# Swin block with a mixture of experts on one core: one order of work for all engines replaced by a table for each engine, one product moved to GpSimd

## The chip, the cores and the metric

One NeuronCore of one Trainium2 chip runs the whole program. The metric is the device time of one execution in microseconds (us), from the first to the last instruction with what lies around them. Engines are named as the profile names them: PE (TensorE, the matmuls; PEld its weight loads), DVE (VectorE), ACT (ScalarE), POOL (GpSimd) and SP (SyncE, which here only issues DMAs).

## The reference

The input is 16 images of 56x56 positions with 32 channels, in float32. Two residual blocks follow each other:

```
x = x + window_attention(layernorm(x))      # 7x7 windows, shifted by 3, 4 heads of 8 channels
x = x + experts(layernorm(x))               # 8 experts of 32x32, the best 2 of each position

attention: q, k, v = h @ w_qkv + b_qkv
           a = softmax(q k^T * 8**-0.5) + bias + mask   # bias and mask come after the softmax
           out = (a v) @ w_proj + b_proj
experts:   p = softmax(h @ router_w + router_b); the two largest p, divided by their sum
           out = p1 * (h @ We1 + be1) + p2 * (h @ We2 + be2)
```

## The kernel before

**Units.** The work is cut into 16 units. A unit is half the columns of two images, 4 columns of windows by 8 rows of windows by 2 images: 64 windows, in 112 partitions of x and 28 windows' columns by 32 channels along the free axis. Every unit passes through the same steps, each step a function of the name in the tables:

- `load` (SP, 12 DMAs into the single tile `xin`), `keep` (SP, one DMA from `xin` to `x_kept`, of which there are two), `kept` (POOL, adds the projection's bias to `x_kept`).
- `norm1_center`, `norm1_square`, `norm1_scale`, `norm1_root`: the first layernorm, which goes DVE (sum, L893), POOL (centre, L558), ACT (square), DVE (sum), ACT (logarithm and exponential), DVE (root), POOL (scale, L567). `norm2_*` does the same for the second one.
- `xt`, `q`, `k`, `v`: PE turns the rows and projects them, ACT copies the results to SBUF. `place` and `kmask` spread q and k by heads (POOL L593 and L630, ACT L733). `ob` is bias and mask times v.
- Attention runs in four groups g of 16 windows. For each: `maximum` (PE products into `ps_win`, L1213; DVE maximum of each row, L943, and its split, L957 and L959), `shift` (PE turns the maxima, L1221; ACT copies them to `mr`, L778), `scores` (PE, L1236 and L1242, into the same `ps_win`; ACT exponential to `pt`, L788), `pv` (PE products with v, L1258; DVE divides by the sums, L966 and L970; POOL adds `ob`, L601). There is one `ps_win`, so `maximum` of a group can't start before the exponentials of the group before it are read out.
- `ot`, `y`, `back`: PE turns and projects, DVE adds `x_kept` (L984) and so makes `x2`.
- `x2t`, `route`, `logits`: PE and ACT. `top2` picks the two largest in six pieces: pieces 0 to 4 on DVE (L999 to L1034), piece 5 on POOL. `share` turns the shares of the experts.
- `replicate` (SP): the normed tokens are copied by DMA to the four groups of partitions (tile `x4`). `gates` (SP): shares go to DRAM in 4 DMAs and come back spread over partitions in 8 DMAs, 4 for experts 0 to 3 (semaphore `gates_low`) and 4 for experts 4 to 7 (`gates_high`).
- `mul` (DVE, L1046): four products of `gates` with `x4`, pieces 0 to 3; pieces 0 and 2 are 448 columns wide and 1 and 3 are 336, times 4. Pieces 0 and 1 use the low experts, 2 and 3 the high ones. `sum` (PE) adds the experts in `ps_acc`, `mix_drain` (ACT), `final` (PE, DVE L1054), `store` (SP, 12 DMAs).

**Order.** All five engines walk one list, `program()`: each engine takes from it the steps in which it has a part, in that order, and runs them strictly one after the other. The list is a prologue, then for each unit one macro step with places (g, 0) to (g, 3), where `SIDE_TASKS` says which steps of other units stand, then a tail. In the macro step of unit n, attention is that of n, `xt` to `ob` and `keep` that of n+1, `load` and the first norm that of n+2, `y` to `top2` piece 2 that of n-1, the rest that of n-2. `back` stands at places (0, 2) and (0, 3), `keep` ahead of it at (0, 0), `load` at (0, 1), `norm1_center` of the next unit at (1, 0), and `maximum` of group 2 after it.

`keep` of unit n+1 waits until `back` of unit n-1 has read the same `x_kept`, and `load` waits until `keep` has emptied `xin`:

```
sp.wait_ge(token_drained, upto("token_drained", v.before(2), 1))      # keep
sp.wait_ge(x_kept_ready, upto("x_kept_ready", v.before(1)))           # load
dve.wait_ge(x_loaded, upto("x_loaded", v))                            # norm1_center on DVE
```

PE's small products share two PSUM banks in turn (`FILL_ORDER`): a fill waits until the fill two before it is read out.

## Time and profile before

| | |
|---|---|
| median of 3 runs | 995.84 us (995.42 to 998.39) |
| the profiled execution's own time | 994.43 us |
| its span, first to last instruction | 992.6 us |
| busy share of the span | PE 67%, PEld 43%, DVE 59%, ACT 38%, POOL 40% |
| mean granted TensorE clock | 0.753 of full speed |
| DMA moved | 100.79 MB, mean 102 GB/s |

No engine is busy for much over two thirds of the span. The busy time of PE depends on the clock that it was granted, since the same matmuls take longer at the lower one. The chain that ended last passes through PE for 34% of the span, DVE 23%, DMA 14%, "issue" (time in which the engine waited for nothing that the profile shows) 10%, ACT 8% and SP's queue 7%.

### The profile page before, as it was taken

What the parts mean: (1) busy time and instruction counts of PE and PEld (TensorE: products, weight loads), DVE (VectorE), ACT (ScalarE), POOL (GpSimd) and SP (SyncE); (2) the same over time, 40 slices, a digit from 0 to 9 for tenths busy, and PEclk for the clock granted to TensorE, in tenths of its full rate; (3) what the DMA queues carried; (4) which work ended last, traced back from release to release, by engine and by line L of the source; (5) the groups of instructions that cost most, each with busy time, mean ns of one, the idle gap of its engine ahead of it and who ended that gap; (6) DMA issues with size and microseconds to landing.
All of it is one profiled execution on the core that took longest, in us unless ns stands there. A gap on an engine that the chain in (4) does not pass through costs nothing.

```text
span 992.6 us, 28757 instructions
## 1 busy us (share of the span) xinstructions
PE 664.2 (67%) x12210; PEld 431.4 (43%) x12210; DVE 582.7 (59%) x878; ACT 376.8 (38%) x737; POOL 401.1 (40%) x458
## 2 busy tenths in 40 slices
PE   3777675768577574867758486876767677866423
PEld 1455453545345353545435354554445445543200
DVE  6342556737476673847577484656758466666433
ACT  2444443343344334435333443534344344422200
POOL 3442525444362544436254443625344362621200
PEclk9777595957969587877768788776968678786655
DMA  3001127355281735528173552817364371845664
GB/s 104 18 4 34 35 52 157 75 128 106 56 187 49 159 69 124 116 64 182 42 155 71 126 114 64 181 48 154 67 145 98 85 157 50 185 101 117 132 146 104
DMA packets 40511, 100.79 MB, mean 102 GB/s; under 512 B 12736, under 2 KB 14784, under 8 KB 38848
## 3 DMA queue, kind: packets, MB, share of 16 engines
q1 hardware_dynamic: 39952, 98.05, 44.8%
q8 instruction: 97, 1.59, 0.7%
q10 hardware_dynamic: 432, 0.90, 0.3%
q14 instruction: 30, 0.25, 0.1%
HBM read 58.78 MB, written 8.03 MB: 67 GB/s over the span
## 4 chain that ended last, share of the span: by engine, by line
PE 34%; DVE 23%; DMA 14%; issue 10%; ACT 8%; SPq 7%; POOL 3%; ACTq 0%; DVEq 0%; POOLq 0%
PE ps_pv L1258 7%; DMA gates<-shares_kept 6%; SPq L487 5%; DVE mx L943 5%; DMA x_kept<-xin 5%; PE ps_win L1242 5%; PE ps_win L1213 4%; PE ps_shared L1278 4%; PE ps_acc L1334 3%; DVE gates L1046 3%; ACT pt L788 3%; PE ps_shared L1293 2%; DVE x L984 2%; PE ps_shared L1167 2%; DMA xin<-x 2%
## 5 line engine op out<-in xcount | busy, mean ns | idle before, releaser
L601 POOL TENSOR_TENSOR on<-on,obs 128x256 f32<-128x256 f32 x64 | 77.8, 1215 | 221.0 <-DVE on L970 186.6
L1046 DVE TENSOR_TENSOR gates<-gates,x 128x1792 f32<-128x1792 f32 x64 | 118.2, 1854 | 74.7 <-DMA gates<-shares_kept 73.8
L943 DVE TENSOR_REDUCE mx<-ps_win 128x32 f32<-128x1568 f32 x64 | 114.4, 1788 | 62.2 <-PE ps_win L1213 55.3
L788 ACT ACTIVATE pt<-ps_win 128x784 f32<-128x784 f32 x128 | 98.4, 821 | 111.2 <-PE ps_win L1242 111.2
L1258 PEld LDWEIGHTS ps_pv<-vb,pt 128*49 128x49 f32 x4096 | 124.0, 149 | 24.2 <-issue 22.3
L1258 PE MATMUL ps_pv<-vb,pt 128*49 128x18 f32 x4096 | 130.6, 214 | 1.7 <-issue 1.7
L1334 PE MATMUL ps_acc<-gates,folded_tile 128*32 128x336 f32 (+1 forms) x512 | 74.7, 669 | 67.8 <-DVE gates L1046 60.3
L1213 PE MATMUL ps_win<-kbd,qp 32*49 32x196 f32 x2048 | 76.9, 421 | 35.2 <-ACT pt L788 33.6
L1242 PE MATMUL ps_win<-qbd,kp 32*49 32x196 f32 x2048 | 96.4, 442 | 0.4 <-issue 0.4
L1221 PE MATMUL ps_win<-const_bf_tile,ms 128*128 128x128 bf16 x256 | 33.2, 271 | 79.8 <-DVE ms L959 79.6
L893 DVE TENSOR_REDUCE st<-xin 112x28 f32<-112x896 f32 x16 | 17.4, 1085 | 109.6 <-DMA xin<-x 109.6
L1236 PE MATMUL ps_win<-mr,const_bf_tile 32*49 32x196 bf16 x1024 | 43.7, 316 | 53.7 <-ACT mr L778 53.5
L593 POOL TENSOR_SCALAR qbd<-qp,const_tile 128x392 f32<-128x392 f32 x128 | 77.3, 617 | 0.0
L1213 PEld LDWEIGHTS ps_win<-kbd,qp 32*49 32x49 f32 x2048 | 41.6, 149 | 79.2 <-ACT pt L788 69.6
L1221 PEld LDWEIGHTS ps_win<-const_bf_tile,ms 128*128 128x128 bf16 x256 | 20.9, 120 | 108.8 <-DVE ms L959 89.2
L567 POOL TENSOR_TENSOR xc<-xc,st 112x896 f32<-112x896 f32 x16 | 27.1, 1696 | 93.1 <-DVE st L912 93.1
L630 POOL TENSOR_SCALAR kbd<-kp,const_tile 128x392 f32<-128x392 f32 x64 | 58.3, 928 | 0.0
L745 ACT COPY vb<-ps_shared 49x512 f32<-49x512 f32 x64 | 37.9, 593 | 39.6 <-PE ps_shared L1177 39.2
L1236 PEld LDWEIGHTS ps_win<-mr,const_bf_tile 32*49 32x49 bf16 x1024 | 18.6, 122 | 78.2 <-ACT mr L778 69.9
L1242 PEld LDWEIGHTS ps_win<-qbd,kp 32*49 32x49 f32 x2048 | 48.4, 156 | 7.8 <-issue 1.2
L1167 PE MATMUL ps_shared<-xt,folded_tile 64*64 64x392 f32 x256 | 38.6, 683 | 19.0 <-DVE x L984 15.6
L1334 PEld LDWEIGHTS ps_acc<-gates,folded_tile 128*32 128x32 f32 x512 | 11.7, 122 | 90.7 <-DVE gates L1046 51.8
(95 smaller groups left out, 1188.2 us busy)
## 6 DMA issues: line engine op xcount, KB each, us to landing
gates<-shares_kept SPq DMA_DIRECT2D x128, 392.0 KB, 9.8
x<-x SPq DMA_DIRECT2D x48, 392.0 KB, 5.0
x_kept<-xin SPq DMA_DIRECT2D x16, 392.0 KB, 3.4
x<-x2t SPq DMA_DIRECT2D x64, 98.0 KB, 2.8
xin<-x SPq DMA_DIRECT2D x32, 150.0 KB
out<-xo SPq DMA_DIRECT2D x32, 150.0 KB
shares_kept<-shares SPq DMA_DIRECT2D x64, 24.5 KB, 1.5
xin<-x SPq DMA_DIRECT2D x32, 18.0 KB
```

Source lines behind the costliest of these rows:

```text
L593: nc.gpsimd.tensor_scalar(qbd[i][:, :, h, :], qp[v.par][:, 8 * i:8 * i + 8, :], head_rows[:, h:h + 1], 1.0, ALU.mult, ALU.mult).then_inc(q ...
L601: nc.gpsimd.tensor_tensor(o, o, obs[u.par][:, g, :, :, :, :].rearrange("p k a h d -> p (k a h d)"), ALU.add).then_inc(o_ready, 1)
L630: ins = nc.gpsimd.tensor_scalar(kbd[i][:, :, h, :], kp[v.par][:, 8 * i:8 * i + 8, :], head_rows[:, h:h + 1], 1.0, ALU.mult, ALU.mult)
L788: nc.scalar.activation(pt[g % 2][:, k, :, :, :].rearrange("p a h n -> p a (h n)"), ps_win[:, :, HN * k:HN * k + HN], ACT.Exp).then_inc(pro ...
L943: nc.vector.tensor_reduce(mx[g % 2].rearrange("n a x h -> n a (x h)"), ps_win[:, :, 0:8 * N].rearrange("n a (k m) -> n a k m", m=N), AX, A ...
L1046: nc.vector.tensor_tensor(gate, gate, x4[w.par][:, :, columns(half)], ALU.mult).then_inc(gated, 1)
L1167: ins = mm(halves[b][to:to + 64, 0:HALF], w64[rows, rows], xt[rows, 8 * b:8 * b + 8, :, :].rearrange("p q k i -> p (q k i)"), start=True, ...
L1213: ins = mm(ps_win[PAD * k:PAD * k + N, a, HN * x:HN * x + HN], qp[u.par][r, q, :], kbd[g // 2][r, q % 8, :, :].rearrange("p h n -> p (h n) ...
L1236: mm(ps_win[PAD * k:PAD * k + N, a, HN * x:HN * x + HN], shift_sel[r, x, :], mr[g % 2][r, :, k, 0:N], start=True, stop=False)
L1242: ins = mm(ps_win[PAD * k:PAD * k + N, a, HN * x:HN * x + HN], kp[u.par][r, q, :], qbd[g // 2][r, q % 8, :, :].rearrange("p h n -> p (h n) ...
L1258: ins = mm(ps_pv[PAD * x:PAD * x + N, c0:c0 + SLOT], pt[g % 2][:, x, place, h, :], vb[u.par][:, 2 * g + x, a, h, :], start=True, stop=True)
L1334: ins = mm(ps_acc[C * a:C * a + C, 0:n], we[:, eh, :], gates[:, eh, a, columns(half)], start=(eh == 0), stop=(eh == 1), skip_group_check=True)
```

## The change

Each engine gets its own list of steps: `FIRST`, then `STEPS` for each of 15 steps, then `LAST`. An entry (name, i, ahead) in `STEPS` is piece i of unit step + ahead; entries with a unit below 0 are left out. So the order on one engine no longer follows from that on another, and an engine's step may begin and end at another place of the unit than its neighbour's.

Four things go with it:

- the semaphores that counted several kinds of work together (`pre_filled`, `pre_drained`, `token_filled`, `token_drained`) become one pair for each kind of work;
- the scratch tile `sq` of the two norms becomes two tiles, and the logarithm gets a row of its own in `st1` and `st2` (row 5);
- `mul` piece 3 (336 x 4 columns) runs on POOL with a semaphore of its own, `gated_pool`, which PE's last `sum` waits for;
- SP's `replicate` and `gates` are cut in two and three tasks, so that the wait between the first DMAs and the rest needn't stop the queue at one place.

No other arithmetic, shape or DMA changes. The core of the diff (the lists `FIRST` and `LAST` are shown in part, `LAST` by DVE's; the renamed semaphores are left out):

```diff
-NORM1 = ("load", "norm1_center", "norm1_square", "norm1_scale")
-PRE_ORDER = ("norm1_root", "keep", "kept", "xt", "q", "k", "place", "kmask", "v", "ob")
-LATE = ("share", "gates", "mul", "sum", "mix_drain", "final", "store")
-SIDE_TASKS = {
-    (0, 0): [("norm1_root", 0), ("top2", 3), ("top2", 4), ("keep", 0), ("ot", 1), ("xt", 0), ("xt", 1), ("top2", 5)],
-    (0, 1): [("load", 0), ("y", 0)],
-    (0, 2): [("back", 0), ("share", 0), ("q", 0), ("y", 1)],
-    (0, 3): [("back", 1), ("gates", 0), ("norm2_center", 0)],
-    (1, 0): [("k", 0), ("norm1_center", 0)],
-    (1, 1): [("norm2_square", 0)],
-    (1, 2): [("v", 0), ("place", 0), ("norm2_scale", 0)],
-    (1, 3): [("kept", 0), ("norm2_root", 0)],
-    (2, 0): [("kmask", 0), ("norm1_square", 0), ("mul", 0)],
-    (2, 1): [("x2t", 0)],
-    (2, 2): [("x2t", 1), ("norm1_scale", 0), ("mul", 1), ("sum", 0)],
-    (2, 3): [("route", 0), ("replicate", 0), ("mul", 2)],
-    (3, 0): [("v", 1), ("logits", 0), ("sum", 1), ("mix_drain", 0), ("kmask", 1), ("top2", 0)],
-    (3, 1): [("place", 1), ("sum", 2)],
-    (3, 2): [("ob", 0), ("top2", 1), ("mul", 3)],
-    (3, 3): [("ob", 1), ("sum", 3), ("top2", 2), ("mix_drain", 1), ("top2_exp", 0), ("ot", 0), ("final", 0), ("final", 1), ("store", 0)],
+FIRST = {
...
+FIRST = {
...
+}
+
+STEPS = {
+    "SP": [
+        ("gates", 1, -2), ("gates", 2, -2), ("replicate", 0, -1), ("store", 0, -3), ("replicate", 1, -1),
+        ("keep", 0, 2), ("load", 0, 3), ("gates", 0, -1),
+    ],
+    "POOL": [
+        ("norm2_root", 0, -2), ("place", 0, 0), ("pv", 0, -1), ("pv", 1, -1), ("norm1_center", 0, 1), ("pv", 2, -1),
+        ("pv", 3, -1), ("place", 1, 0), ("mul", 3, -3), ("norm1_root", 0, 1), ("kmask", 1, 0), ("top2", 5, -2),
+        ("norm2_center", 0, -1), ("kept", 0, 1),
+    ],
+    "ACT": [
+        ("scores", 1, -1), ("xt", 0, 0), ("share", 0, -3), ("norm2_square", 0, -2), ("xt", 1, 0), ("shift", 2, -1),
+        ("k", 0, 0), ("norm2_scale", 0, -2), ("scores", 2, -1), ("q", 0, 0), ("kmask", 0, 0), ("x2t", 0, -2),
+        ("shift", 3, -1), ("v", 0, 0), ("scores", 3, -1), ("x2t", 1, -2), ("norm1_square", 0, 1), ("route", 0, -2),
+        ("v", 1, 0), ("shift", 0, 0), ("logits", 0, -2), ("ot", 0, -1), ("scores", 0, 0), ("ot", 1, -1),
+        ("norm1_scale", 0, 1), ("ob", 0, 0), ("mix_drain", 0, -3), ("mix_drain", 1, -3), ("ob", 1, 0),
+        ("top2_exp", 0, -2), ("shift", 1, 0),
+    ],
+    "DVE": [
+        ("mul", 2, -3), ("top2", 0, -2), ("top2", 1, -2), ("final", 0, -3), ("top2", 2, -2), ("final", 1, -3),
+        ("norm1_root", 0, 1), ("back", 0, -1), ("back", 1, -1), ("maximum", 1, 0), ("top2", 3, -2), ("top2", 4, -2),
+        ("pv", 0, 0), ("norm2_center", 0, -1), ("maximum", 2, 0), ("norm2_scale", 0, -1), ("pv", 1, 0),
+        ("norm2_root", 0, -1), ("maximum", 3, 0), ("norm1_center", 0, 2), ("pv", 2, 0), ("mul", 0, -2),
+        ("maximum", 0, 1), ("place", 0, 1), ("pv", 3, 0), ("mul", 1, -2), ("norm1_scale", 0, 2),
+    ],
+    "PE": [
+        ("ot", 0, -1), ("shift", 0, 0), ("logits", 0, -2), ("scores", 0, 0), ("ot", 1, -1), ("sum", 0, -3),
+        ("ob", 0, 0), ("maximum", 1, 0), ("sum", 1, -3), ("final", 0, -3), ("sum", 2, -3), ("sum", 3, -3),
+        ("final", 1, -3), ("y", 0, -1), ("y", 1, -1), ("ob", 1, 0), ("pv", 0, 0), ("shift", 1, 0), ("scores", 1, 0),
+        ("xt", 0, 1), ("xt", 1, 1), ("maximum", 2, 0), ("share", 0, -2), ("pv", 1, 0), ("shift", 2, 0), ("k", 0, 1),
+        ("scores", 2, 0), ("q", 0, 1), ("maximum", 3, 0), ("v", 0, 1), ("x2t", 0, -1), ("pv", 2, 0), ("shift", 3, 0),
+        ("scores", 3, 0), ("x2t", 1, -1), ("v", 1, 1), ("maximum", 0, 1), ("route", 0, -1), ("pv", 3, 0),
+    ],
+}
+
+LAST = {
...
+    "DVE": [
+        ("top2", 13, 0), ("mul", 12, 2), ("top2", 13, 1), ("top2", 13, 2), ("final", 12, 0), ("top2", 13, 3),
+        ("top2", 13, 4), ("final", 12, 1), ("back", 14, 0), ("pv", 15, 0), ("maximum", 15, 1), ("back", 14, 1),
+        ("norm2_center", 14, 0), ("maximum", 15, 2), ("norm2_scale", 14, 0), ("norm2_root", 14, 0), ("mul", 13, 0),
+        ("maximum", 15, 3), ("pv", 15, 1), ("mul", 13, 1), ("pv", 15, 2), ("mul", 13, 2), ("top2", 14, 0),
+        ("top2", 14, 1), ("pv", 15, 3), ("top2", 14, 2), ("top2", 14, 3), ("final", 13, 0), ("top2", 14, 4),
+        ("final", 13, 1), ("back", 15, 0), ("back", 15, 1), ("norm2_center", 15, 0), ("norm2_scale", 15, 0),
+        ("norm2_root", 15, 0), ("mul", 14, 0), ("top2", 15, 0), ("top2", 15, 1), ("top2", 15, 2), ("top2", 15, 3),
+        ("top2", 15, 4), ("mul", 14, 1), ("mul", 14, 2), ("mul", 15, 0), ("mul", 15, 1), ("final", 14, 0),
+        ("final", 14, 1), ("mul", 15, 2), ("final", 15, 0), ("final", 15, 1),
+    ],
...
-def program():
...
+def program(engine):
+
+    for name, number, i in FIRST[engine]:
+        yield name, Unit(number), i
+    for step in range(UNITS - 1):
+        for name, i, ahead in STEPS[engine]:
+            if 0 <= step + ahead < UNITS:
+                yield name, Unit(step + ahead), i
+    for name, number, i in LAST[engine]:
+        yield name, Unit(number), i
+
+
...
-        sq = sb("sq", [ROWS, WS, A, C])
-        st1 = sb("st1", [ROWS, 5, TOK])
+        sq1, sq2 = (sb(n, [ROWS, WS, A, C]) for n in ("sq1", "sq2"))
+        st1 = sb("st1", [ROWS, 6, TOK])
...
-            def replicate(w, _):
-
-                sp.wait_ge(token_drained, upto("token_drained", w, 3))
-                if w.has_before(2):
-                    sp.wait_ge(gated, upto("gated", w.before(2)))
+            def replicate(w, i):
+
                 x4p = x4[w.par]
-                for a in range(A):
-                    sp.dma_start(x4p[0:C, a, :], x2t[C * a:C * a + C, :]).then_inc(x4_first, 16)
-                sp.wait_ge(x4_first, upto("x4_first", w))
-                for e in range(1, 4):
-                    sp.dma_start(x4p[C * e:C * e + C, :, :].rearrange("p a t -> p (a t)"),
-                                 x4p[0:C, :, :].rearrange("p a t -> p (a t)")).then_inc(x4_ready, 16)
-
-            def gate_rows(w, _):
-
-                sp.wait_ge(shares_drained, upto("shares_drained", w))
-                if w.has_before(1):
-                    sp.wait_ge(gates_low, upto("gates_low", w.before(1)))
-                    sp.wait_ge(gates_high, upto("gates_high", w.before(1)))
-                for b in range(4):
-                    sp.dma_start(shares_kept[:, BLOCK * b:BLOCK * b + BLOCK],
-                                 shares[32 * b:32 * b + 32, :]).then_inc(shares_stored, 16)
+                if i == 0:
+                    sp.wait_ge(x2t_drained, upto("x2t_drained", w))
+                    if w.has_before(2):
+                        sp.wait_ge(gated, upto("gated", w.before(2)))
+                        sp.wait_ge(gated_pool, upto("gated_pool", w.before(2)))
+                    for a in range(A):
+                        sp.dma_start(x4p[0:C, a, :], x2t[C * a:C * a + C, :]).then_inc(x4_first, 16)
+                else:
+                    sp.wait_ge(x4_first, upto("x4_first", w))
+                    for e in range(1, 4):
+                        sp.dma_start(x4p[C * e:C * e + C, :, :].rearrange("p a t -> p (a t)"),
+                                     x4p[0:C, :, :].rearrange("p a t -> p (a t)")).then_inc(x4_ready, 16)
+
+            def gate_rows(w, i):
+
+                if i == 0:
+                    sp.wait_ge(shares_drained, upto("shares_drained", w))
+                    if w.has_before(1):
+                        sp.wait_ge(gates_low, upto("gates_low", w.before(1)))
+                        sp.wait_ge(gates_high, upto("gates_high", w.before(1)))
+                    for b in range(4):
+                        sp.dma_start(shares_kept[:, BLOCK * b:BLOCK * b + BLOCK],
+                                     shares[32 * b:32 * b + 32, :]).then_inc(shares_stored, 16)
+                    return
                 sp.wait_ge(shares_stored, upto("shares_stored", w))
                 if w.has_before(1):
                     sp.wait_ge(mixed, upto("mixed", w.before(1)))
-                for eh in range(2):
-                    for e in range(4):
-                        rows = bass.AP(shares_kept.tensor, shares_kept.offset + (4 * eh + e) * COLS,
-                                       [[0, C], [E * COLS, A], [1, COLS]])
-                        sp.dma_start(gates[C * e:C * e + C, eh, :, :], rows).then_inc(gates_high if eh else gates_low, 16)
+                eh = i - 1
+                for e in range(4):
+                    rows = bass.AP(shares_kept.tensor, shares_kept.offset + (4 * eh + e) * COLS,
+                                   [[0, C], [E * COLS, A], [1, COLS]])
+                    sp.dma_start(gates[C * e:C * e + C, eh, :, :], rows).then_inc(gates_high if eh else gates_low, 16)
 
...
+            def mul(w, _):
+
+                pool.wait_ge(x4_ready, upto("x4_ready", w))
+                pool.wait_ge(gates_high, upto("gates_high", w))
+                gate = gates[:, 1, :, columns(1)]
+                nc.gpsimd.tensor_tensor(gate, gate, x4[w.par][:, :, columns(1)], ALU.mult).then_inc(gated_pool, 1)
+
...
-                if v.has_before(3):
-                    act.wait_ge(sqsum2, upto("sqsum2", v.before(3)))
-                else:
-                    if v.has_before(1):
-                        act.wait_ge(sqsum1, upto("sqsum1", v.before(1)))
+                if v.has_before(1):
+                    act.wait_ge(sqsum1, upto("sqsum1", v.before(1)))
                 act.wait_ge(centered1, upto("centered1", v))
-                nc.scalar.activation(sq[:, :, :, :], xc1[:, :, :, :], ACT.Square, scale=ROOT_C).then_inc(squared1, 1)
+                nc.scalar.activation(sq1[:, :, :, :], xc1[:, :, :, :], ACT.Square, scale=ROOT_C).then_inc(squared1, 1)
 
             def norm2_square(w, _):
 
-                if w.number + 2 < UNITS:
-                    act.wait_ge(sqsum1, upto("sqsum1", Unit(w.n + 2)))
-                else:
+                if w.has_before(1):
                     act.wait_ge(sqsum2, upto("sqsum2", w.before(1)))
                 act.wait_ge(centered2, upto("centered2", w))
-                nc.scalar.activation(sq[:, :, :, :], xc2[:, :, :, :], ACT.Square, scale=ROOT_C).then_inc(squared2, 1)
+                nc.scalar.activation(sq2[:, :, :, :], xc2[:, :, :, :], ACT.Square, scale=ROOT_C).then_inc(squared2, 1)
 
...
-                pe.wait_ge(gated, upto("gated", w, 2 * eh + half))
+                if eh and half:
+                    pe.wait_ge(gated_pool, upto("gated_pool", w))
+                else:
+                    pe.wait_ge(gated, upto("gated", w, 2 * eh + half))
```

## Rows read from the trace of the kernel before

**Rows 1.** Busy us (instructions) per engine, clock, DMA share, GB/s: one step; eleven steps.
```profile
439.60:497.90 58.30, 40.43 (x755) 26.17 (x751) 37.21 (x53) 23.45 (x46) 25.81 (x28) 0.77 0.48 107
...
sum 641.30, PE 449.56 PEld 294.29 DVE 402.44 ACT 261.36 POOL 287.92; mean PE 40.87 PEld 26.75 DVE 36.59 ACT 23.76 POOL 26.17
```
**Rows 2.** DVE's waits: line, releaser, us in total, times, longest.
```profile
DVE st L893 <- DMA xin<-x: 109.6, 13, 9.3
```
**Rows 3.** The chain that ended last, around 490 us: start, length, what.
```profile
490.44 3.38 DMA x_kept<-xin
...
501.40 1.79 DVE mx L943
```
**Rows 4.** Timeline: DVE behind its wait for xin, PE behind DVE (start, length).
```profile
500.40 1.09 DVE L893 TENSOR_REDUCE st<-xin 112x28 f32<-112x896 f32 x1 [8.91 <-DMA xin<-x]
...
445.85 0.61 PE L1221 MATMUL ps_win<-const_bf_tile,ms 128*128 128x128 bf16 x4 [6.05 <-DVE ms L959]
```
**Rows 5.** Groups of instructions by form, DVE: busy us, mean ns of one.
```profile
L943 DVE TENSOR_REDUCE mx<-ps_win 128x32 f32<-128x1568 f32 x64 | 114.4, 1788 | 62.2 <-PE ps_win L1213 55.3 <-POOL pick L619 4.2 <-POOL mixw L622 2.2
L1046 DVE TENSOR_TENSOR gates<-gates,x 128x1792 f32<-128x1792 f32 x32 | 68.9, 2154 | 74.2 <-DMA gates<-shares_kept 73.8
L1046 DVE TENSOR_TENSOR gates<-gates,x 128x1344 f32<-128x1344 f32 x32 | 49.7, 1554 | 0.5
L1007 DVE TENSOR_TENSOR pick<-tmp,top 98x256 f32<-98x256 f32 x32 | 34.7, 1083 | 1.1
```
**Rows 6.** Groups of instructions by form, POOL.
```profile
L567 POOL TENSOR_TENSOR xc<-xc,st 112x896 f32<-112x896 f32 x16 | 27.1, 1696 | 93.1 <-DVE st L912 93.1
...
L618 POOL TENSOR_TENSOR pick<-pick,top 98x256 f32<-98x256 f32 x16 | 10.1, 630 | 49.1 <-DVE top L1034 49.1
```
**Rows 7.** Timeline: DVE and POOL over each other; the last row with POOL idle.
```profile
449.19 2.57 DVE L938 SCALAR_TENSOR_TENSOR st<-st 112x28 f32<-112x28 f32 x1
449.64 2.07 POOL L640 TENSOR_TENSOR x_kept<-x_kept,weight_tile 112x896 f32<-112x896 f32 x1
...
458.91 2.97 POOL L601 TENSOR_TENSOR on<-on,obs 128x256 f32<-128x256 f32 x1 [5.38 <-DVE on L970]
...
944.38 0.42 DVE L1007 TENSOR_TENSOR pick<-tmp,top 98x256 f32<-98x256 f32 x1
```
**Rows 8.** Timeline, PE: one group's products at the upper clock, the last at the lower.
```profile
461.81 0.67 PE L1242 MATMUL ps_win<-qbd,kp 32*49 32x196 f32 x16
...
464.70 0.91 PE L1213 MATMUL ps_win<-kbd,qp 32*49 32x196 f32 x32
...
466.71 1.65 PE L1258 MATMUL ps_pv<-vb,pt 128*49 128x18 f32 x64
...
454.84 2.86 PE L1258 MATMUL ps_pv<-vb,pt 128*49 128x18 f32 x64
```
**Rows 9.** Groups of instructions by form, ACT: the two of the attention chain.
```profile
L788 ACT ACTIVATE pt<-ps_win 128x784 f32<-128x784 f32 x128 | 98.4, 821 | 111.2 <-PE ps_win L1242 111.2
...
L778 ACT COPY mr<-ps_win 128x512 bf16<-128x512 bf16 x64 | 37.5, 586 | 32.0 <-PE ps_win L1221 31.4
```
**Rows 10.** Timeline: SP's issues of a load and of gates, and the products behind them.
```profile
493.88 5.18 SPq L487 DMA_DIRECT2D xin<-x  x12
...
444.08 3.90 SPq L526 DMA_DIRECT2D gates<-shares_kept  x8
...
453.86 2.03 DVE L1046 TENSOR_TENSOR gates<-gates,x 128x1792 f32<-128x1792 f32 x1 [2.09 <-DMA gates<-shares_kept]
...
461.73 2.04 DVE L1046 TENSOR_TENSOR gates<-gates,x 128x1792 f32<-128x1792 f32 x1 [0.43 <-DMA gates<-shares_kept]
```
**Rows 11.** Busy time by stretches of 2 us: PE at the lower clock.
```profile
446.00:448.00 2.00, 0.46 (x4) 0.19 (x2) 1.42 (x2) 0.50 (x2) 1.48 (x4) 0.50 0.99 238
```
**Rows 12.** Group 3's copy to mr: unit 0 (chain), unit 15 (timeline).
```profile
65.33 0.58 ACT mr L778
...
905.99 0.59 ACT L778 COPY mr<-ps_win 128x512 bf16<-128x512 bf16 x1 [1.74 <-PE ps_win L1221]
```

More of the change, by code:

```diff
@@ L62 @@
 TRANSFERS = 2 * len(ROW_CUTS) * len(COL_CUTS)
-PRE_FILLS = 10
 TOP2_STEPS = 18
@@ L666, in _ @@
                     kept(unit, i)
+                elif step == "mul" and i == 3:
+                    mul(unit, i)
                 elif step == "top2" and i == 5:
@@ L1098, in _ @@
             ones(vb[0])
-            for step, unit, i in program():
+            for step, unit, i in program("DVE"):
                 if step == "norm1_center":
```

240 lines of the change are left out of this document (131 added, 109 removed), and 7 rows, old and new, of tables (LAST, TAIL).

## The prediction

> **What bounds the kernel now.** I read the busy times by stretches first. One step (a unit's worth of work in steady state) takes 58.3 us, and over eleven such steps PE is busy for 40.9 us of it, DVE 36.6, POOL 26.2 and ACT 23.8, the DMA engines for half of it [rows 1]. Nothing is full. PE's 40.9 holds much work at the lower clock: the granted clock averages 0.77 in these steps, so the same matmuls at the upper one would take no less than 31.5 us.
>
> The tight loop inside a step is that of the attention groups, because there is one `ps_win`: scores (twice 0.67 us, [rows 8]), two exponentials of 0.82 [rows 9], the products for the maxima 0.91 [rows 8], their reduction 1.79 [rows 5], its split and the turn on PE (0.6 at the lower clock, [rows 4]; about 1.1 together), the copy to `mr` 0.59 [rows 9]. That is about 7.4 us, 30 us in four groups. So a step of 58.3 is bound neither by an engine nor by this loop, but by what the one order makes engines wait for.
>
> The waits name the largest: DVE's first reduction of `norm1_center` waited 109.6 us in all, in 13 places, for `xin` [rows 2]. The chain shows why: it leaves `back` at 490.4 us, goes through the copy to `x_kept` (3.4 us), SP's issues of the twelve loads and the transfer, and is back on DVE with a maximum at 501.4 [rows 3]. That maximum (of group 2) needs nothing of `xin`; it only stands behind `norm1_center` on DVE, which sat idle for 8.9 us, and PE behind the maximum for 6.05 [rows 4]. Then the clock is down: at 446 to 448 us the granted clock is 0.50, that is 1.2 GHz [rows 11], and 64 products of `pv` take 2.86 us in place of 1.65 at 2.4 GHz [rows 8].
>
> **The change, part by part.** *DVE's order.* `keep` and `load` still follow `back` on SP, but DVE now meets `norm1_center` of that unit only after maximum 3, with maxima 1, 2 and 3, two pieces of `top2`, two `pv` and the second norm in between. By my walk `back` ends 17 us into the new step, the load's last issue is 0.5 + 3.4 + 5.2 us later [rows 3, 10], the data are there at 27, and DVE asks for them at 35. The wait of 8.9 us is gone with 8 us to spare.
>
> *What replaces it.* I walked the new tables through one steady step with durations of the groups, PE at the upper clock, time 0 at the end of PE's products for maximum 0. DVE has nearly all its older work between maximum 0 and 1: `pv` 3, `mul` 1, a reduction, `mul` 2, three pieces of `top2`, both `final`, the root, both `back`. Maximum 1's products are ready at 9 us and DVE takes them at 17, so the attention loop waits for DVE there, but DVE works all the time. The scores of the four groups begin at 4, 20, 28 and 37 us: after the first, groups follow each other at about 8 us, near the loop's 7.4. So DVE becomes the bound. The sum for a step:
> 36.6 us, DVE's busy time now [rows 1];
> - 1.55 us, the `mul` piece that leaves [rows 5];
> + 1.5 us between instructions of DVE (53 in a step [rows 1], some 0.03 each; an estimate);
> + 4.6 us of waits that the walk leaves on DVE: 1.5 at `mul` 0 for the gates, 1.4 before maximum 3 for PE and ACT, 0.8 at the second norm's root for ACT, 0.9 elsewhere;
> + 4.4 us of extra blocking between DVE and POOL (below).
> That gives 45.6 us a step.
>
> *The gates.* They are asked for one position earlier than they are needed, but are no longer covered by much. After `top2` piece 4, POOL's piece 5, the turn, ACT, the store of the shares and 9.8 us from the first issue of gates to the first product [rows 10] make some 16 us; DVE has 14 us of other work until `mul` 0. `mul` 2 needs the high half, 17.7 us after the first issue [rows 10], and stands in the next step, where I see 3 us to spare.
>
> *`mul` 3 on POOL.* No row shows it. POOL's product of 256 columns takes 0.63 us and of 896 1.70 [rows 6]; that line gives 2.44 us for 1344. From below it could cost what DVE takes, 1.55; from above its 2.44 and a wait like L601's, which stretched to 2.97 [rows 7]. POOL's load rises from 26.2 to 28.6 in 45.6 us, and PE wants the result at 12 us of the step where POOL has it at 9 to 10.5, so its length is hidden. What isn't hidden is the blocking. A DVE instruction of 28 columns took 2.57 us and ended when POOL's addition to `x_kept` did; DVE's L1007 takes 0.42 with POOL idle [rows 7] and 1.08 on the mean [rows 5]. Twice 0.66 and one such 2.4 make 3.7 us of DVE's time a step now. POOL is busy 45% of a step, and 62% after it, which adds 1.4 us by proportion; and in the walk `mul` 3 on POOL lies over `mul` 2 and the first pieces of `top2` on DVE, and costs up to 2.4 once, with about 0.6 where `mul` 1 meets `place`. I take 4.4 together; below it could be nothing, if the tables happen to keep them apart. So this part alone is worth 1.55 less about 3: it takes nothing off, and may cost a us or two. The Trainium skill says the same more strictly ("SBUF — State Buffer", Who interferes with whom): a DVE instruction with two SBUF inputs and a GpSimd instruction that reads SBUF exclude each other for their whole length. The trace agrees in the rows named. Its page "GPSIMD Engine Reference" (section 3.1) has 4497 ns for 2048 elements, from which I would estimate 2.95 us here; the sum would stay as it is.
>
> *PE.* PE's last long idle stretch goes, so more of it should run at the upper clock. It needs 31.5 to 40.9 us of 45.6. I take no further gain and no loss.
>
> *SP.* In a step it issues 20-odd us of DMAs and waits for about 5; `load` stands ahead of the shares' store. By the walk the load's issues end at 25.6 and the shares are ready at 25.0, so 0.6 us is lost, inside the 1.5. The split of `replicate` only puts the store into a gap. The semaphores, the second `sq` and the extra row cost nothing; they are what allows the orders.
>
> **The sum.** From the copy of group 3 of unit 0 to that of unit 15 there are now 840.7 us for 15 steps [rows 12]. After: two light steps (no sums, at first no `top2`) of 38 and 40 us, estimates between the loop's 30 and the full step, and 13 of 45.6: 671. The front, 65.3 us [rows 12], stays. The end, 86.6 us from that copy to the end of the span of 992.6, stays a matter of two gate trips one after the other; I take 84. That is 820 us of span. The profiled execution lies 1.8 above its span, and the median 1.4 above that execution: 823 us. Less than 0.3% (3 us) of this kernel can't be told from no change.
>
> **Rivals.**
> *The wait comes back as a wait for gates.* If the shares' store stands on SP behind `keep` and `load` in full (9.1 us, [rows 3, 10]) and not 0.6 us, `mul` 0 waits 7 to 8 us more, with maximum 0 behind it on DVE, as today's maximum 2. 13 steps of 7.6 give 922 us. It decides if `back` slips by several us against `top2` 4. Beside it, that nothing but `xin`'s wait goes: 995.8 - 109.6 = 886. Together 0.27, for 870 to 930.
> *Faster still.* If the blocking adds nothing, 13 times 4.4 less: 766 us; the upper clock throughout would help. 0.14, under 785.
> *Slower: the block between DVE and POOL.* If every us of POOL held DVE, a step would be DVE's 36.6 - 3.7 - 1.55, POOL's 28.6 and 1.5: 61.5 us, and the kernel 1030 us. It passes today's time once the blocking costs 21 us a step in place of my 8. Against it: reductions such as L943 hold 1.79 on the mean while POOL works [rows 5]. The page named above speaks for it only as far as two-input instructions go, a third of DVE's time. 0.07.
> *No change*: only if gates and blocking together eat all, 0.02.
> The likeliest, 785 to 870, has 0.50. The range of 770 to 915 leaves out about 1 in 10 on either side. Faster 0.91.
>
> **What would show it.** In the profile after: DVE's wait for `xin` under 20 us in all; DVE busy over 75% of the span and first in the chain; steps of 43 to 49 us; POOL's L1046-like product at 2.4 us or more; L1007 and L938 longer than now; DVE's waits for gates in steady state 1 to 3 us a step; granted clock over 0.8. I am wrong if the gates' wait is 7 us a step, if PE falls to the lower clock in each step, or if ACT's waits for a norm (it takes the square ahead of the `shift` copy) open gaps in the attention loop that the walk doesn't have.

## The result, and the profile after

| | before | after |
|---|---|---|
| median | 995.63 us (991.2 to 998.39) | 857.27 us (855.47 to 857.52, and one of 2563.17) |
| span of the profiled execution | 992.6 us | 853.6 us |
| mean granted TensorE clock | 0.753 | 0.834 |
| step in steady state (third to fifteenth start of the second norm's first sum, 12 steps) | 56.8 us | 48.5 us |

The ratio is 0.8608 [0.8567, 0.8649]: 13.9% faster, where 17.3% were forecast. The twelfth interval of before is a short one (47.1 us); the eleven ahead of it average 57.7 us, against the 58.3 that the prediction took. In after, the same eleven average 48.3. The execution of 2563.17 us is a disturbed one; it counts in the median and not in the ratio.

The page of after, its first lines. They answer to the busy shares in the table of before:

```profile
span 853.6 us, 28829 instructions
...
PE 614.8 (72%) x12210; PEld 409.7 (48%) x12210; DVE 570.1 (67%) x862; ACT 369.1 (43%) x737; POOL 473.8 (56%) x474
...
POOL 29%; issue 25%; PE 21%; DVE 15%; ACT 4%; DMA 3%; SPq 2%; POOLq 0%; DVEq 0%; ACTq 0%
```

The last of them is the chain that ended last, by engine. It does not begin with DVE, as forecast, but with POOL.

DVE's waits over the whole of after (releaser, us in total, times, longest), the view of [rows 2]:

```profile
DVE mx L995 <- PE ps_win L1265: 123.4, 47, 9.9
DVE xo L1106 <- PE ps_shared L1339: 41.7, 29, 6.0
DVE gates L1098 <- DMA gates<-shares_kept: 33.8, 7, 19.2
DVE st L985 <- ACT st L859: 24.1, 16, 2.1
```

`xin` is no longer in the list; before it stood there with 109.6 us. The wait for gates is almost all in the tail (one of 19.2 us). The first row is new as a leader: a maximum (L995, L943 of before) waits for PE's products.

Busy time in fifteen stretches of 46.84 us each, from group 3's copy of unit 0 on (the view of [rows 1]; one stretch in the middle, and the sum):

```profile
481.78:528.62 46.84, 35.52 (x817) 24.78 (x814) 35.82 (x53) 24.08 (x49) 30.34 (x29) 0.96 0.55 124
...
sum 702.60, PE 543.32 PEld 370.01 DVE 501.39 ACT 334.32 POOL 423.31; mean PE 36.22 PEld 24.67 DVE 33.43 ACT 22.29 POOL 28.22
```

Nothing is full here either. The groups of DVE and POOL in the stretch from 200 to 750 us, that is 11.3 steps (busy us, mean ns of one, then idle before it):

```profile
L995 DVE TENSOR_REDUCE mx<-ps_win 128x32 f32<-128x1568 f32 x46 | 82.3, 1788 | 78.8 <-PE ps_win L1265 78.7
L1098 DVE TENSOR_TENSOR gates<-gates,x 128x1792 f32<-128x1792 f32 x22 | 56.7, 2579 | 3.3 <-DMA gates<-shares_kept 3.3
L1009 DVE TENSOR_SCALAR ms<-mx 128x32 bf16<-128x32 f32 x45 | 36.5, 811 | 1.5
L1052 DVE TENSOR_TENSOR tmp<-logits,top 98x256 f32<-98x256 f32 x22 | 19.6, 890 | 0.8
...
L1106 DVE TENSOR_TENSOR xo<-ps_shared,x 112x384 f32<-112x384 f32 (+1 forms) x23 | 14.3, 622 | 28.3 <-PE ps_shared L1339 28.3
...
L1059 DVE TENSOR_TENSOR pick<-tmp,top 98x256 f32<-98x256 f32 x23 | 9.8, 425 | 0.8
```

```profile
L685 POOL TENSOR_TENSOR gates<-gates,x 128x1344 f32<-128x1344 f32 x11 | 35.1, 3191 | 0.0
...
L637 POOL TENSOR_TENSOR turn<-plus_c 1x1 f32<-1x1 f32 x22 | 26.7, 1213 | 0.5
```

What the reader is to see: the blocking between DVE and POOL (the lock, in short: one engine's instruction is held while the other's runs) has moved. L1059 (L1007 of before, 1083 ns [rows 5]) is back to 425. L1009, the first half of the split of the maxima and so a step of the attention chain, works on 32 elements; it took 0.24 us where POOL stood still (at 456.03 us) and takes 811 ns on the mean. The wide products of `mul` (L1098, L1046 of before) are held longer too: 2579 ns in place of 2154 [rows 5].

The chain in one step. The timeline of POOL first, then of PE and DVE (start, length, idle before in brackets):

```profile
486.57 1.97 POOL L647 TENSOR_TENSOR on<-on,obs 128x256 f32<-128x256 f32 x1 [5.58 <-DVE on L1022]
488.50 2.42 POOL L637 TENSOR_TENSOR turn<-plus_c 1x1 f32<-1x1 f32 x1
490.91 2.90 POOL L639 TENSOR_SCALAR qbd<-qp,const_tile 128x392 f32<-128x392 f32 x4
493.77 3.19 POOL L685 TENSOR_TENSOR gates<-gates,x 128x1344 f32<-128x1344 f32 x1
```

```profile
497.01 0.77 PE L1391 MATMUL ps_acc<-gates,folded_tile 128*32 128x336 f32 x8 [1.98 <-POOL gates L685]
498.44 0.71 PE L1339 MATMUL ps_shared<-const_tile,ym 128*112 128x128 f32 x3 [0.65 <-ACT ym L890]
498.94 3.19 PE L1332 MATMUL ps_shared<-weight_tile,ot 128*112 128x128 f32 x14
```

On POOL `mul` 3 stands behind an addition, a 1x1 instruction that took 2.42 us and ended with DVE's `mul` 2 (488.87 to 490.89 us), and the four of `place`. PE waits for it; `final`, `y`, `back` and DVE's maximum 1 (at 502.65 us) then follow one behind the other.

### The profile page after: what moved, and what is told of

The parts are those of the page before. It is cut to its first block, busy times and chain, and to the rows that moved or that the text cites. A ratio compares the mean times of both kernels' runs of the same rounds, so it can differ in the third digit from the quotient of the medians.

```text
span 853.6 us, 28829 instructions
## 1 busy us (share of the span) xinstructions
PE 614.8 (72%) x12210; PEld 409.7 (48%) x12210; DVE 570.1 (67%) x862; ACT 369.1 (43%) x737; POOL 473.8 (56%) x474
## 4 chain that ended last, share of the span: by engine, by line
POOL 29%; issue 25%; PE 21%; DVE 15%; ACT 4%; DMA 3%; SPq 2%; POOLq 0%; DVEq 0%; ACTq 0%
POOL qbd L639 7%; DVE mx L995 5%; POOL on L647 5%; POOL gates L685 4%; PE ps_acc L1391 4%; PE ps_shared L1332 3%; POOL turn L637 3%; POOL xc L621 2%; PE ps_win L1265 2%; PE ps_pv L1312 2%; PE ps_win L1294 2%; POOL xc L630 2%; DVE ms L1009 2%; DMA gates<-shares_kept 2%; PE ps_shared L1339 1%
## 5 line engine op out<-in xcount | busy, mean ns | idle before, releaser
L995 DVE TENSOR_REDUCE mx<-ps_win 128x32 f32<-128x1568 f32 x64 | 114.5, 1789 | 123.5 <-PE ps_win L1265 123.4
L1098 DVE TENSOR_TENSOR gates<-gates,x 128x1792 f32<-128x1792 f32 (+1 forms) x48 | 104.6, 2182 | 33.9 <-DMA gates<-shares_kept 33.8
L1312 PE MATMUL ps_pv<-vb,pt 128*49 128x18 f32 x4096 | 113.8, 203 | 6.6 <-issue 5.4
L1312 PEld LDWEIGHTS ps_pv<-vb,pt 128*49 128x49 f32 x4096 | 108.8, 131 | 20.1 <-issue 15.0
L1391 PE MATMUL ps_acc<-gates,folded_tile 128*32 128x336 f32 (+1 forms) x512 | 69.3, 628 | 44.0 <-DVE gates L1098 23.8
L830 ACT COPY mr<-ps_win 128x512 bf16<-128x512 bf16 x64 | 37.5, 586 | 113.7 <-PE ps_win L1273 113.7
L630 POOL TENSOR_TENSOR xc<-xc,st 112x896 f32<-112x896 f32 x16 | 27.1, 1696 | 69.5 <-DVE st L990 69.5
L685 POOL TENSOR_TENSOR gates<-gates,x 128x1344 f32<-128x1344 f32 x16 | 52.4, 3275 | 22.4 <-DMA gates<-shares_kept 22.3
L613 POOL TENSOR_TENSOR xc<-xc,st 112x896 f32<-112x896 f32 x16 | 27.2, 1697 | 60.0 <-DVE st L964 60.0
L890 ACT COPY ym<-ps_acc 128x448 f32<-128x448 f32 (+1 forms) x32 | 15.5, 486 | 100.2 <-PE ps_acc L1391 100.2
L808 ACT COPY obs<-ps_shared 128x256 f32<-128x256 f32 x64 | 20.7, 375 | 79.3 <-PE ps_shared L1244 79.3
L1009 DVE TENSOR_SCALAR ms<-mx 128x32 bf16<-128x32 f32 x64 | 49.9, 779 | 2.2
L1229 PE MATMUL ps_shared<-folded_tile,xt 128*49 128x128 f32 x512 | 44.8, 330 | 4.2 <-issue 3.6
```

Source lines behind the costliest of these rows:

```text
L685: nc.gpsimd.tensor_tensor(gate, gate, x4[w.par][:, :, columns(1)], ALU.mult).then_inc(gated_pool, 1)
L995: nc.vector.tensor_reduce(mx[g % 2].rearrange("n a x h -> n a (x h)"), ps_win[:, :, 0:8 * N].rearrange("n a (k m) -> n a k m", m=N), AX, A ...
L1009: nc.vector.tensor_scalar(hi, m, -1.0, None, ALU.mult).then_inc(shift_rounded, 1)
L1098: nc.vector.tensor_tensor(gate, gate, x4[w.par][:, :, columns(half)], ALU.mult).then_inc(gated, 1)
L1229: ins = mm(bank[PAD * g:PAD * g + N, 128 * j:128 * j + 128], keys, wv, start=True, stop=True)
L1312: ins = mm(ps_pv[PAD * x:PAD * x + N, c0:c0 + SLOT], pt[g % 2][:, x, place, h, :], vb[u.par][:, 2 * g + x, a, h, :], start=True, stop=True)
```

## Experiments

Line numbers are those of after, or of before for its variants; in the run that lightens POOL they are 4 higher. Ratios are to the kernel before.

**1. One entry back: the first norm's sums behind `back`.** The kernel after, on DVE alone:

```diff
-("maximum", 3, 0), ("norm1_center", 0, 2), ("pv", 2, 0)
+("maximum", 3, 0), ("pv", 2, 0)
-("back", 1, -1), ("maximum", 1, 0)
+("back", 1, -1), ("norm1_center", 0, 2), ("maximum", 1, 0)
```

> The changed kernel with one entry of DVE's table moved: norm1_center stands right behind the second back again, ahead of maximum 1, as in the kernel before. If DVE's wait for xin at the head of its queue was the largest thing that the tables removed, a step grows from 48.3 us by 8 to 9 us (the copy to x_kept, twelve issues, the transfer), which comes to about 970 us, DVE waits over 100 us for xin, and the granted clock falls from 0.83 towards 0.77. The rival, that the gain comes from the packing of the other work and that this one wait would be filled by slack elsewhere, expects under 20 us more (up to 877).

Measured: 1011.46 us, ratio 1.0111 [1.0041, 1.0181]; a step of 59.1 us. DVE's waits, and the chain:

```profile
DVE mx L995 <- PE ps_win L1265: 172.8, 48, 9.8
DVE st L945 <- DMA xin<-x: 118.9, 13, 9.7
```

```profile
434.16 0.57 DVE x L1036
434.80 3.35 DMA x_kept<-xin
...
442.20 1.54 DMA xin<-x
443.80 0.97 issue
444.76 1.79 DVE mx L995
```

One entry of 27 on one engine gives back the whole gain and more, 154 us, some 11 us a step (the profiled execution took 1022.8 us, so its step is about 1% long). I had expected 113. The chain is that of [rows 3] again: `back`, `x_kept`, the twelve loads, `xin`, and a maximum that needs none of it. The two kernels differ in which: before it is maximum 2, here maximum 1, so in this run three maxima of the unit come behind the wait and not two. This shows that the place of `norm1_center` is necessary to the gain. Whether it is enough, the next four runs on the kernel before ask.

**2. The same place in one common order.** The kernel before, its list of side tasks:

```diff
-    (1, 0): [("k", 0), ("norm1_center", 0)],
+    (1, 0): [("k", 0)],
...
-    (2, 1): [("x2t", 0)],
+    (2, 1): [("x2t", 0), ("norm1_center", 0)],
```

with `norm1_square` and `norm1_scale` moved from group 2 to places (3, 0) and (3, 2).

> The kernel before with its one order kept for all engines and only the first norm's tasks of the next unit moved one group back (norm1_center from place (1,0) to (2,1), norm1_square to (3,0), norm1_scale to (3,2)). If the wait for xin alone made the step long, this goes from 995.6 to 870-890 us, and the tables as such are worth only 15 to 30 us more. The rival says that in a common order the stall comes back in another place (the norm's chain is now late for xt, or PE's and DVE's other waits grow): then it stays over 930 us.

Measured: 1005.5 us, ratio 1.0082 [1.0048, 1.0117]. DVE's wait for `xin` is gone, and DVE's first product waits instead:

```profile
DVE gates L1046 <- DMA gates<-shares_kept: 140.1, 18, 11.6
```

SP in that step issued the load at 492.17 us (4.35 us of it), the shares' store at 496.63, the gates at 499.46, and the product began at 509.79 after 10.68 us of waiting. My theory is wrong and its rival holds: the time comes back in full. The wait for DMA does not: 109.6 us for `xin` are gone and the wait for gates grew by 66 (from 73.8 [rows 5]); DVE's maxima now wait 121.3 us for PE where they waited 55.3.

**3. SP's gates ahead of keep and load.** Run 2, and

```diff
-    (0, 1): [("load", 0), ("y", 0)],
+    (0, 1): [("y", 0)],
-    (0, 3): [("back", 1), ("gates", 0), ("norm2_center", 0)],
+    (0, 3): [("back", 1), ("gates", 0), ("keep", 0), ("load", 0), ("norm2_center", 0)],
```

with `keep` gone from place (0, 0).

> The kernel before with one order for all engines: the first norm's tasks one group later (as in the run before it) and, on SP, keep and load behind gates in place of ahead of them. The run before it showed DVE's wait for xin come back as a wait of about 10 us for the gates, which SP issues behind the twelve loads. The theory that the step is bound by SP's one queue between back and DVE (xin and the gates can't both be in time while load stands ahead of gates and mul 0 ahead of maximum 3) expects both waits gone: 870 to 905 us. The rival, that a common order can't be relieved at one place because another wait always takes over, expects over 960 us.

Measured: 1005.13 us, ratio 1.0114 [1.0088, 1.0139]. The time comes back once more, and the largest wait for DMA now stands in POOL's queue:

```profile
POOL x_kept L640 <- DMA x_kept<-xin: 87.2, 13, 9.9
```

POOL's `kept` stands there ahead of the second norm's root, so PE's `x2t` (L1293) waited 83.4 us in all for POOL, and what stands behind it in the other queues with it. `xin`, loaded later here, is not wholly in time either: DVE waits 44.3 us for it, and 23.8 for the gates.

**4. `kept` late too.** Run 3, with `kept` and `norm1_center` at place (2, 3), `norm1_square` at (3, 1), `norm1_scale` at (3, 3):

```diff
-    (1, 3): [("kept", 0), ("norm2_root", 0)],
+    (1, 3): [("norm2_root", 0)],
...
-    (2, 3): [("route", 0), ("replicate", 0), ("mul", 2)],
+    (2, 3): [("route", 0), ("replicate", 0), ("kept", 0), ("norm1_center", 0), ("mul", 2)],
```

> The kernel before, still one order for all engines, with four moves: the sums of norm1_center late, keep and load behind the gates on SP (both as in the run before it), and now also POOL's kept moved from the second group to the third, with norm1_center, norm1_square and norm1_scale a place or two later still. In the run without the last move the wait had gone into POOL's queue at kept (87 us in all) and from there to x2t on PE. Theory 'each wait needs only its own place; a common order can be relieved too': no wait for xin, for gates or at kept is longer than 2 us a step, 880 to 920 us. Rival 'in a common order a place that is late enough for one engine is too late for another': the waits go once more to another place (norm1_root at the next step's start, or xt on PE), 960 us or more.

Measured: 957.44 us, ratio 0.962 [0.9539, 0.9701]; a step of 54.4 us. DVE over the whole run:

```profile
L1046 DVE TENSOR_TENSOR gates<-gates,x 128x1792 f32<-128x1792 f32 x64 | 116.6, 1828 | 23.7 <-DMA gates<-shares_kept 23.2
L943 DVE TENSOR_REDUCE mx<-ps_win 128x32 f32<-128x1568 f32 x64 | 114.7, 1792 | 143.7 <-PE ps_win L1213 140.4 <-POOL pick L619 2.9
...
L893 DVE TENSOR_REDUCE st<-xin 112x28 f32<-112x896 f32 x16 | 17.3, 1083 | 25.5 <-DMA xin<-x 25.4
```

In time it is nearly the rival, in mechanism nearly the theory: the waits for DMA are down to 49 us from the 183 of before (109.6 [rows 2] and 73.8 [rows 5]), so a common order can be relieved of them. But 135 us of such waits taken away bring 38 us: DVE's maxima wait 140 us for PE where they waited 55 [rows 5].

**5. `mul` 3 back on DVE.** The kernel after, with `mul` 3 behind `mul` 2 on DVE and off POOL:

```diff
-("place", 1, 0), ("mul", 3, -3), ("norm1_root", 0, 1)
+("place", 1, 0), ("norm1_root", 0, 1)
-("mul", 2, -3), ("top2", 0, -2)
+("mul", 2, -3), ("mul", 3, -3), ("top2", 0, -2)
```

> The changed kernel with mul piece 3 back on DVE, right behind piece 2. The lock theory (piece 3 on POOL takes 3.3 us and stretches what DVE does beside it) expects the same time within 1%, 850 to 866 us: DVE gets 1.55 us of work more a step and loses less in blocked instructions, and PE's last sum no longer waits for POOL. The rival, that the part is worth its 1.55 us a step because DVE is the bound, expects 20 us more (877).

Measured: 829.59 us, ratio 0.8296 [0.8242, 0.835]; a step of 46.5 us. DVE from 200 to 750 us:

```profile
L995 DVE TENSOR_REDUCE mx<-ps_win 128x32 f32<-128x1568 f32 x47 | 84.1, 1789 | 82.8 <-PE ps_win L1265 82.7
L1009 DVE TENSOR_SCALAR ms<-mx 128x32 bf16<-128x32 f32 x47 | 36.3, 772 | 1.6
...
L1106 DVE TENSOR_TENSOR xo<-ps_shared,x 112x512 f32<-112x512 f32 (+1 forms) x24 | 15.0, 624 | 4.1 <-PE ps_shared L1339 3.4
```

On POOL the product thus costs 28 us, 2.0 us a step; the first theory expected nothing of it, and the second that it saves 20. L1009 is as long as before the edit, so the lock in the attention chain was not `mul` 3's doing; what went is the wait of `final` for PE, 28.3 to 3.4 us, and with it the chain through POOL.

**6. `mul` 3 on POOL in the kernel before.** One part alone.

> The kernel before with mul piece 3 on POOL and nothing else changed. DVE isn't the bound there, so both theories expect little; the lock theory expects 990 to 1000 us, with the product on POOL at 2.4 to 3.3 us, and the rival (1.55 us a step off DVE's path) 970 to 975 us.

Measured: 1009.04 us, ratio 1.0114 [1.0046, 1.0182]. It costs some 12 us where the order is otherwise untouched, which neither theory had (990 to 1000 and 970 to 975 us). POOL's product took 3407 ns on the mean, and PE's sums:

```profile
L1348 PE MATMUL ps_acc<-gates,folded_tile 128*32 128x336 f32 (+1 forms) x512 | 73.5, 658 | 78.9 <-POOL gates L641 44.6 <-DVE gates L1057 26.2 <-ACT ym L849 7.9
```

**7. `mul` 3 ahead of `place` on POOL.** The kernel after, with

```diff
-("place", 1, 0), ("mul", 3, -3), ("norm1_root", 0, 1)
+("mul", 3, -3), ("place", 1, 0), ("norm1_root", 0, 1)
```

> The changed kernel with mul piece 3 still on POOL, but ahead of place piece 1 in its table instead of behind it. If what piece 3 costs on POOL is that PE's last sum, both y and back wait for it in the queue behind place (4 instructions, 2.9 us), this gives back most of the 28 us that moving it to DVE gave: 830 to 840 us. If it is the blocking between DVE and POOL that costs, wherever the product stands, it stays at 850 us or more.

Measured: 846.03 us, ratio 0.8501 [0.847, 0.8532]. So 11 of the 28 us come back, though the wait of `final` for PE is gone in full (0.7 us from 200 to 750, where it was 28.3). What is left goes with the lock. The product, now over DVE's `mul` 2, took

```profile
L685 POOL TENSOR_TENSOR gates<-gates,x 128x1344 f32<-128x1344 f32 x16 | 77.5, 4845 | 22.5 <-DMA gates<-shares_kept 22.4
```

in place of 3275 ns on the mean, while L637 fell from 1032 to 260 ns. At 478.49 us it took 5.29, with DVE's `mul` 2 beside it from 478.85 to 480.86: the 2.01 us of that product come on top of its own. In turn it holds DVE's `top2` behind `mul` 2:

```profile
L1052 DVE TENSOR_TENSOR tmp<-logits,top 98x256 f32<-98x256 f32 x22 | 33.3, 1516 | 0.8
```

That is from 200 to 750 us; the same instruction took 890 ns in after and 472 in run 5. DVE is busy for 36.5 us a step here without `mul` 3 (418.75 of 550 us at a step of 48.0), and for 35.4 in run 5 with it. `mul` 2 on DVE holds what POOL has there: `mul` 3 in this run, the 1x1 instruction in after and in run 5.

**8. POOL's load taken away.** Run 5, and from the second unit on POOL's spread q, masked k, bias times v and bias onto `x_kept` touch one column, or one token's row, instead of all. The output leaves these terms out.

```diff
-nc.gpsimd.tensor_scalar(qbd[i][:, :, h, :], qp[v.par][:, 8 * i:8 * i + 8, :], ...)
+wide, high = (8, 49) if v.number == 0 else (1, 1)
+nc.gpsimd.tensor_scalar(qbd[i][:, 0:wide, h, 0:high], qp[v.par][:, 8 * i:8 * i + wide, 0:high], ...)
```

> The kernel after with mul 3 on DVE, where from the second unit on POOL's four kinds of wide work in attention and keeping (spread q, masked k, bias times v onto o, bias onto x_kept) touch one column or a few instead of all: the output leaves these terms out. About 178 us of POOL's 310 us busy in the stretch from 200 to 750 us go, and with them their locks on DVE; waits and their order stay. Theory 'lock': DVE's split of the maxima (mean 773 ns, four a step in the attention loop) comes back to 300 to 400 ns, DVE's waits for PE shrink with it, a step of 46 us loses 3 to 4: 775 to 790 us. Rival 'the step is bound by DVE's and PE's own work and the length of the loop, the lock is only where the time shows': L1009 gets shorter, but the time stays within 10 us of 829.6.

Measured: 801.5 us, ratio 0.8041 [0.799, 0.8092], 28 us under run 5; a step of 45.0 us. DVE from 200 to 750 us:

```profile
L1102 DVE TENSOR_TENSOR gates<-gates,x 128x1792 f32<-128x1792 f32 (+1 forms) x49 | 86.8, 1791 | 53.2 <-DMA gates<-shares_kept 53.2
L999 DVE TENSOR_REDUCE mx<-ps_win 128x32 f32<-128x1568 f32 x47 | 84.1, 1788 | 65.2 <-PE ps_win L1269 65.1
...
L1013 DVE TENSOR_SCALAR ms<-mx 128x32 bf16<-128x32 f32 x47 | 11.3, 240 | 1.6
```

The split of the maxima falls to 240 ns, the products of `mul` from 2070 to 1791. DVE's busy time goes from 35.4 us a step (418.87 of 550) to 30.6 (374.08 of 550): 4.8 us were lock. But the step loses 1.5 only. A wait for gates has come up, 53 us in 550, 4.4 a step. The lock theory is right in its mechanism and too high in its price, because the gates' trip is next in line: DVE's wait for gates grows by 4.0 us a step (4.8 us in 550 in run 5), which is more than the 3.3 us that are missing. POOL's own instructions are shorter as well here (213.42 of 550 us busy, 322.92 in run 5), so the 28 us are the most that the lock alone can be worth.

**9. SP's store of the shares ahead of keep and load.** Run 5, SP alone:

```diff
-("keep", 0, 2), ("load", 0, 3), ("gates", 0, -1),
+("gates", 0, -1), ("keep", 0, 2), ("load", 0, 3),
```

> The kernel after with mul 3 on DVE, and SP's store of the shares (gates 0) ahead of keep and load in each step instead of behind them. The prediction gave 0.6 us a step to their present order. Theory 'slack on both sides': neither xin (8 us of slack) nor the gates (3.3 us of waits in 11 steps) gain or lose, 825 to 835 us. Rival 'the tables hold only in this order': SP then waits for the shares with the load behind them, DVE waits for xin again by 3 us or more a step, above 860 us.

Measured: 852.5 us, ratio 0.8551 [0.8499, 0.8603], about 23 us more than run 5. Neither theory holds: there is slack for `xin` (5.6 us of waits in all), but none for the gates (124.6 us in 26 waits). SP's timeline:

```profile
510.90 2.58 SPq L562 DMA_DIRECT2D shares_kept<-shares  x4
513.58 0.54 SPq L535 DMA_DIRECT2D x_kept<-xin  x1
516.99 4.54 SPq L528 DMA_DIRECT2D xin<-x  x12
521.63 3.80 SPq L572 DMA_DIRECT2D gates<-shares_kept  x8
```

The load now stands between the shares' store and their reading back: 10.7 us from one first issue to the other, where run 5 had 3.2 (496.07 and 499.31 us). Putting the first half of a trip earlier lengthened the trip.

**10. PE kept busy.** Run 5, with 8 products of no use behind each turn of the maxima and 12 ahead of the last sum.

> The changed kernel with mul piece 3 on DVE (829.6 us, clock 0.863) and 44 useless small bf16 matmuls more a step on PE, 8 behind each shift turn and 12 ahead of the last sum, into columns that nobody reads; the result is unchanged. If the lower clock is what separates steps of 51 us from those of 45, more activity lifts the granted clock to over 0.9 and takes 10 to 25 us off (805 to 820). If the clock only follows from the waits, or fillers delay real matmuls as much as they help, the time stays at 825 us or rises.

Measured: 837.4 us, ratio 0.8412 [0.8391, 0.8433]. The mean granted clock rose from 0.863 to 0.883, from 200 to 750 us from 0.88 to 0.91, and the time by some 8 us. These fillers cost more than the clock gave; other numbers or places of them were not tried.

**11. The tail.** Run 5, with `top2` of unit 15 ahead of `mul` 14 on DVE, and on SP `gates` 2 of unit 14 and `store` 13 ahead of `replicate` 15.

> The changed kernel with mul piece 3 on DVE and another end: DVE takes all of top2 of unit 15 ahead of the products of unit 14, and SP issues gates 14 high and store 13 ahead of unit 15's spreading, so that nothing stands between unit 15's shares and its gates. The end (from group 3 of unit 15 on, 90.7 us in the changed kernel) is two gate trips in a row; if the second starts with the shares of unit 15, it comes 4 to 8 us earlier: 822 to 826 us. If it waits for the sums of unit 14 instead, nothing changes (828 to 831).

Measured: 826.38 us, ratio 0.8308 [0.8255, 0.8361]: not to be told from run 5 (0.8296) by its interval. In the profiled executions the end, from the copy to `mr` of group 3 of unit 15 on, is 85.9 us long where run 5 has 90.1, so the order of the end does what it was meant to, in size within the 4 to 8 us expected, but the spread of the whole time hides it. Of the versions that compute everything it has the lowest median, by 3 us.

## Why the prediction was right, and where it wasn't

**The direction and the cause** held: 857 lies in the range and among the likeliest (785 to 870), the step of 48.5 us in my 43 to 49, DVE no longer waits for `xin`, and run 1 shows that without this one place there is no gain; runs 2 to 4 show that the place alone does not make it. DVE's busy share is 67%, not over 75, and it is not first in the chain. The steps one by one:

**DVE's order: right.** "The wait of 8.9 us is gone with 8 us to spare." It is gone, and run 9, in which the load stands behind the shares' store, brought it back only as 5.6 us in all.

**The rival "the wait comes back as a wait for gates": right for a common order, wrong for this change.** Runs 2, 3 and 9 show where waits can grow instead: for the gates behind the loads in SP's queue, in POOL's queue at `kept`, and within the gates' trip. In after, DVE waits for gates 3.3 us in 550. The other half of that rival, that nothing but `xin`'s wait goes (886 us), is too high for after. The 110 us of that wait were no measure of its worth: with it gone (run 2) or down to 44 us (run 3) a common order gains nothing, and with it down to 25 (run 4) 38 us. What the separate orders add beyond run 4, some 130 us down to run 5, was not taken apart further; in steady state it is 7.9 us a step, from 54.4 to 46.5, nearly all in DVE's time without work, whose cause stays open: of 550 us DVE was busy 363.69 in run 4 and 418.87 in run 5, which leaves 18.4 us and 11.1 us a step.

**The term of waits was the step that failed, in size.** I summed "4.6 us of waits that the walk leaves on DVE" and 1.5 between instructions. Measured in steady state DVE stood still 13.9 us a step (157.4 of 550 us at 48.5 a step). Three parts of that:
- Maxima wait 6.9 us a step for PE (78.7 us in 550), where I had 1.4. The starts of the maxima of one step were 454.21, 461.56, 471.99 and 483.04: intervals of 7.4, 10.4 and 11.1 us, not "about 8". In the first, POOL had nothing to do beside L1009, and the clock was the upper one. In the second, L1009 took 1.28 us beside POOL's addition to `x_kept` in place of 0.24, PE did `k` (1.58 us) ahead of the scores, so these began 0.8 us after the copy to `mr` was over, and they took 1.95 us, not 1.19, at a granted clock of 0.50 (466 to 468 us; 1.2 GHz), against 1.00 at 457 to 459. That is 2.6 of the 3.1 us over the first interval: 1.0 by the lock, 0.8 by the order on PE, 0.8 by the clock. The rest is the turn (0.61 in place of 0.40 us) and the products for the maxima (1.17 in place of 0.91), both at the lower clock too. Ahead of the turn PE had stood still for 1.70 us behind L1011. All this is read on one step's rows.
- The second norm waits 1.7 us a step for ACT (L985, 18.9 us in 550), where I had 0.8: small gaps of the kind that I had named as a way to be wrong.
- `final` waits 2.5 us a step for PE (28.3 us in 550), the chain through POOL's `mul` 3. Run 5 takes it away.

**The busy time: too high, which covered for the waits.** I had 36.6 less 1.55 plus 4.4, 39.5 us a step; it was 34.6 (392.60 of 550 us). Run 8 gives DVE's work nearly without locks, 30.6 us with `mul` 3. Before had 36.6 us in stretches of 58.3, which is 36.2 in a step of 57.7, so about 5.6 us of lock a step, not the 3.7 that I added up from three instructions; after has 5.5 (34.6 plus 1.55, less 30.6), not 8.1: the tables did keep some of it apart (L1059, L990 at 188 ns in place of 1255, against my "longer than now") and put the rest into the attention chain. Two errors of 5 and 8 us with opposite signs left 2.9 us a step, so that the step came out this near is in part luck. Between the two copies of [rows 12] there are now 702.7 us (60.22 and 762.87), 32 more than forecast; the front is 5 less (60.2), the end 7 more (90.7), and that is the 34 us by which the span is over.

The Trainium skill ("SBUF — State Buffer", Who interferes with whom) has this lock for instructions with two inputs in SBUF and for `tensor_scalar` in its mode that uses both ports, and none for `tensor_reduce`. The trace agrees: of the reductions, the maxima (read from PSUM) took 1.78 to 1.79 us and L971 (read from SBUF) 1.07 to 1.09 throughout; L1022, with only one of its two inputs in SBUF, took 0.42 to 0.43; and L1009, a `tensor_scalar` in SBUF, 0.24 with little of POOL's load (run 8) and 0.8 on the mean with it. In which mode L1009 runs no row shows. The prediction applied the page to two-input instructions only and so left L1009, four times a step in the attention chain, out of its sum. My rival "slower" had the lock hold DVE for every us of POOL, and is false; a step would have been 61.5 us.

**`mul` 3 on POOL: right in sign, wrong in reason.** "It takes nothing off, and may cost a us or two"; it costs 2.0 a step. But I said "its length is hidden", and it isn't: it stands at the head of the chain in the profile above. Its own length was 3.02 us at the least and 3.19 in the median, not the 2.44 of my line through smaller instructions; the estimate from the Trainium skill's "GPSIMD Engine Reference" (section 3.1), 2.95 us, was nearer. My two theories for run 5, 850 to 866 and 877, were both too high: they too took the queue for hidden.

**PE, the clock and SP.** The granted clock rose to 0.834, as said ("over 0.8"); as a lever in its own right, more work on PE didn't pay in the one form tried (run 10). On SP the load's issues ended at 462.04 us and the shares, drained at 462.13, were issued at 462.16: the meeting that the walk had at 25.6 and 25.0. The other order costs some 23 us (run 9).

**The tail.** 84 us forecast, 90.7 measured. DVE's two waits for gates there are 6.8 and 19.2 us. Between them SP issues a store of 4.37 us (at 817.04) ahead of the gates, and `mul` 14 stretched POOL's last piece of `top2` by 3.0 us (2.00 and 2.29 in place of twice 0.63). Run 11 takes the store away, but not the lock (2.47 and 1.82 us), since the products of `mul` 14 now lie right behind `top2`, beside the same two instructions.
